# A fused decoder layer on one core: the second tile's softplus moved to the next batch's first quarter, and the prologue's rotation, loads and copies put in another order

## The chip, the cores and the metric

One core of a Trainium2 chip runs the whole program. The metric is the device time of one execution in microseconds (us); lower is better. The engines are TensorE (PE, its weight loads PEld), VectorE (DVE), ScalarE (ACT), GpSimd (POOL) and SyncE (SP, which only issues DMAs here). Each runs its own list of instructions in program order and waits on semaphores.

## What is computed

Four sequences of 512 tokens with 512 features go through three blocks, each followed by a sum with its input and a layer norm: linear attention in chunks of 128, a selective scan (state space model) that is driven by a context, and a mixture of 64 experts.

```python
x = _layernorm(x + _L0_attn_ref(x, Wq, Wk, Wv, Wo, rms_w))
x = _layernorm(x + _L0_xattn_ref(ctx_1024, x, ...))
x = _layernorm(x + _L0_ffn_ref(x, router_weight, gate_up_proj, down_proj))
...
# inside _L0_xattn_ref, u = silu(conv(in_proj(ctx)) + conv_b)
dt_low, Bm, Cm = jnp.split(x_proj_w @ u, [dt_rank, dt_rank + d_state], axis=1)
dt = jax.nn.softplus(dt_proj_w @ dt_low + dt_proj_b)
state = state * exp(dt * A) + (dt * u) * b      # for each of 512 steps, 512 channels, 16 states
y = sum_n(state * c) + D * u
```

## The kernel before

`mixers` does attention, scan and routing; `experts` runs behind it, from about 760 us on, and isn't touched.

The work of `mixers` is staged in batches b (4) and quarters c (4 in each batch, so t = 4b + c counts 16 quarters). A quarter does one tile of 128 channels of the scan, one chunk of attention, and pieces of other work that are placed between the scan's units by hand. The 512 channels of u are four tiles m = 0..3; quarter c scans tile c. A quarter has 8 units k, and unit n = 32b + 8c + k covers four states of 64 channels in two groups: POOL multiplies dt*u by B into `dbu` (`inputs`, L1122), ACT makes exp(dt*A) into `hst` (`decays`, L854), VectorE scans twice (L1312) and multiplies by C (L1318), TensorE sums the states into `y_ps` (`sum_states`, L426).

Units of half a tile share one spread: `copy_steps` (L399) waits for `dtu_ready`, then issues eight DMAs that copy dt and dt*u from `made` into one of two `rep` buffers, four for each of two groups of rows. `decays` and `inputs` of a spread's first unit wait until all of them have landed (`copied`). All copies are issued by SP, but for the second group of the very first spread, which ACT issues.

dt of a tile is a softplus, in steps that go from engine to engine: `project_dt` (TensorE, L455), `soften` (ACT, L874 and L876), `exponentials` (L883, L886), `rounded` (L896), `logs` (L892), `soft_parts` (two POOL instructions, L1128 and L1129), `excess` (ACT, L900), `soft_rest` (POOL, L1134), `steps` (ACT, L904, a ramp), `steps_of_u` (POOL, L1140, dt*u, which raises `dtu_ready`). For b >= 1 tiles 0 and 1 (EARLY) are made in the last quarter of the batch before, tiles 2 and 3 (LATE) in quarters 0 and 1 of their own. For batch 0 tile 0 is made in the prologue, its last steps on VectorE (`first_steps`, L1347 to L1359), and tile 1 in quarter 0.

TensorE's results other than `y_ps` go through three PSUM buffers used in turn (`to_fill`): the use number k waits until the use k - 3 has been emptied. The prologue is written out: four products of the context, the first tap, convolution and SiLU that give u, q0, the product of u (`project_u`), dt of tiles 0 and 1, k0, v0; POOL rotates q0 and k0 (`rotate`, L1195 to L1199), TensorE turns them (L476), ACT copies the result (`qT0`, `kT0`) and makes the first decays.

## Time and profile before

| | us |
|---|---|
| median of 3 runs | 1326.63 |
| lowest, highest | 1321.89, 1329.96 |
| the profiled execution, its own time | 1328.6 |
| its span, first to last instruction | 1326.8 |

| engine | busy us | share |
|---|---|---|
| PE | 1141.6 | 86% |
| DVE | 1112.4 | 84% |
| POOL | 969.8 | 73% |
| ACT | 848.2 | 64% |

The engines' shares are over the whole span; `experts` is 567 us of it. The mean granted clock of TensorE is 0.889 of 2.4 GHz. Starts of scans are the best clockwork of `mixers`: the first scan of a quarter is unit 8c + 0, and the first scans of the batches start at 46.23, 208.79, 383.08 and 564.85 us.

### The profile page before, as it was taken

Reading aid. Unit: us, or ns where it says so; the run is one execution under the profiler, and the core shown is the slowest. Engines: PE = TensorE matmul, PEld = TensorE weight load, DVE = VectorE, ACT = ScalarE, POOL = GpSimd, SP = SyncE. Lnnn points to the kernel's source line nnn. Section 1 sums busy time; section 2 is a strip of 40 time slices with the busy share of each in tenths; the row PEclk is TensorE's granted clock in tenths of the full one; section 3 lists DMA queues with packets and bytes.
Section 4 is the critical chain, followed back from the end, with each engine's and each line's share of the span. In section 5 each row is a group of like instructions: output and inputs, shape, how many; then the busy total and the mean of one; then the engine's idle time right before and its main releaser. Section 6 shows DMA issues by size and latency. Waiting matters only on the chain. (4 is left out here: it accounts for less than half of the span.)

```text
span 1326.8 us, 19363 instructions
## 1 busy us (share of the span) xinstructions
PE 1141.6 (86%) x6421; PEld 764.8 (58%) x6421; DVE 1112.4 (84%) x1564; ACT 848.2 (64%) x1522; POOL 969.8 (73%) x760
## 2 busy tenths in 40 slices
PE   8579998899978979887897749999999999999950
PEld 3334333444433533344443439999989999999940
DVE  3679998989978899788899658998988988988947
ACT  5564585745756446566345338888878888888833
POOL 0688678978999998999895224877767777777644
PEclk9689998898979879887987659999999999999985
DMA  8337326332253332243322337999999999999988
GB/s 303 77 80 240 73 60 158 111 79 54 54 139 80 112 84 49 65 112 111 72 53 96 100 103 215 315 304 308 299 297 305 307 291 305 301 302 311 288 137 333
DMA packets 95138, 235.03 MB, mean 177 GB/s; under 512 B 18608, under 2 KB 18864, under 8 KB 94400
## 3 DMA queue, kind: packets, MB, share of 16 engines
q1 hardware_dynamic: 64128, 161.92, 40.5%
q0 software_dynamic: 30720, 71.36, 22.6%
q8 instruction: 52, 0.85, 0.3%
q10 hardware_dynamic: 192, 0.52, 0.2%
q14 instruction: 46, 0.38, 0.1%
HBM read 147.33 MB, written 52.85 MB: 151 GB/s over the span
## 5 line engine op out<-in xcount | busy, mean ns | idle before, releaser
L1122 POOL TENSOR_TENSOR dbu<-rep,bc 128x1024 f32<-128x1024 f32 x128 | 303.0, 2370 | 62.2 <-PE y_ps L426 27.3
L1312 DVE TENSOR_TENSOR_SCAN hst<-hst,dbu 128x512 f32<-128x512 f32 x256 | 299.1, 1214 | 53.2 <-POOL dbu L1122 42.7
L1786 POOL DMA_INDIRECT sum_rows<-ye,tokens x128 | 204.5, 1598 | 101.0 <-ACT ye L1862 78.7
L1778 POOL DMA_INDIRECT xe<-x_rows,tokens x128 | 152.2, 1189 | 74.8 <-issue 37.8
L426 PE MATMUL y_ps<-dbu,cs 128*32 128x512 f32 x512 | 157.5, 699 | 55.6 <-DVE dbu L1318 43.6
L854 ACT ACTIVATE hst<-rep,small_sb 128x512 f32<-128x512 f32 x256 | 165.9, 685 | 54.5 <-DVE dbu L1318 43.0
L464 PE MATMUL ring<-first_raw,xT 128*128 128x512 f32 x384 | 177.7, 607 | 1.0 <-DVE x L1399 1.0
L1318 DVE TENSOR_TENSOR dbu<-hst,bc 128x1024 f32<-128x1024 f32 x128 | 156.7, 1224 | 4.4
L1828 PE MATMUL low<-xh,w1h 128*128 128x256 f32 x512 | 150.8, 295 | 0.0
L1828 PE MATMUL low<-xl,w1h 128*128 128x256 f32 x512 | 145.5, 284 | 0.0
L1828 PE MATMUL low<-xh,w1l 128*128 128x256 f32 x512 | 145.4, 284 | 0.0
L464 PEld LDWEIGHTS ring<-first_raw,xT 128*128 128x128 f32 x384 | 70.1, 192 | 97.1 <-issue 97.1
L1938 DVE TENSOR_TENSOR w1l<-first_raw,w1h 128x1024 fp32r<-128x1024 f32 (+1 forms) x128 | 117.0, 956 | 9.8 <-ACT w1h L1880 1.2
L1931 DVE TENSOR_TENSOR xl<-turn,xh 128x512 fp32r<-128x512 f32 x128 | 82.6, 686 | 32.8 <-ACT xh L1872 31.8
L1880 ACT ACTIVATE w1h<-first_raw 128x1024 fp32r<-128x1024 f32 (+1 forms) x128 | 101.0, 844 | 5.6 <-PEq L160 5.6
L1828 PEld LDWEIGHTS low<-xl,w1h 128*128 128x128 f32 x512 | 99.0, 193 | 0.0
L1828 PEld LDWEIGHTS low<-xh,w1l 128*128 128x128 f32 x512 | 98.8, 193 | 0.0
L1828 PEld LDWEIGHTS low<-xh,w1h 128*128 128x128 f32 x512 | 98.8, 193 | 0.1
L426 PEld LDWEIGHTS y_ps<-dbu,cs 128*32 128x32 f32 x512 | 20.2, 115 | 120.6 <-DVE dbu L1318 56.5
L485 PEld LDWEIGHTS ring<-qT,kT 32*128 32x128 f32 x512 | 47.7, 272 | 62.8 <-ACT qT L829 33.3
L1816 PE MATMUL turn<-cs,xe 128*128 128x128 f32 x512 | 68.8, 278 | 14.1 <-DMA xe<-x_rows,tokens 13.3
L1195 POOL TENSOR_TENSOR rot<-qk,cs 128x512 f32<-128x512 f32 x32 | 40.4, 1284 | 52.0 <-ACT qk L829 52.0
(208 smaller groups left out, 2726.6 us busy)
## 6 DMA issues: line engine op xcount, KB each, us to landing
first_raw<-in_gate_up SPq DMA_DIRECT2D x64, 768.0 KB, 9.8
rep<-made SPq DMA_DIRECT2D x252, 128.0 KB
second_raw<-in_down SPq DMA_DIRECT2D x64, 256.0 KB, 5.5
bc<-bc_rows SPq DMA_DIRECT2D x64, 128.0 KB, 3.1
second_raw<-in_down SPq DMA_DIRECT2D x64, 128.0 KB, 7.4
rows<-sum_rows SPq DMA_DIRECT2D x16, 512.0 KB, 9.6
sum_rows<-x2T SPq DMA_DIRECT2D x1, 4608.0 KB, 16.6
xT<-in_x_turned SPq DMA_DIRECT2D x16, 256.0 KB, 3.1
```

Source lines behind the costliest of these rows:

```text
L426: ins = pe.matmul(y_ps[rows, :], sel, dbu[:, n % WORK, g, :], start=(k == 0), stop=(k == QUADS - 1))
L464: ins = pe.matmul(ps[:, :], xT[:, t % 2, k, :], wqkv[:, "qkv".index(name), k, :], start=(k == 0), stop=(k == KD - 1))
L854: act.activation(hst[:, at % HBANKS, :], rep[:, i % 2, g, 0, :], ACT.Exp, scale=a_sc[:, 4 * m + 2 * half + g, k:k + 1]).then_inc(da_ready, 1)
L1122: pool.tensor_tensor(dbu[:, n % WORK, :, :], rep[:, i % 2, :, 1, :], bc[:, k, 0, :].unsqueeze(1).broadcast_to([P, 2, T]), ALU.mult).then_i ...
L1312: dve.tensor_tensor_scan(h, h, dbu[:, n % WORK, i, :], 0.0, ALU.mult, ALU.add).then_inc(scanned, 1)
L1318: dve.tensor_tensor(dbu[:, n % WORK, :, :], hst[:, first:first + 2, :], bc[:, k, 1, :].unsqueeze(1).broadcast_to([P, 2, T]), ALU.mult).the ...
L1778: pool.indirect_dma_start(xe[:, e % RAW, j, :], None, x2_dram, bass.IndirectOffsetOnAxis(ap=tokens[:, e, j:j + 1], axis=0))\
L1786: pool.indirect_dma_start(sum_dram[e % SUMS], bass.IndirectOffsetOnAxis(ap=tokens[:, e, j:j + 1], axis=0), ye[:, e % YE, j, :], None, comp ...
L1828: ins = pe.matmul(dst, w[:, s, k, at:at + P], x[:, s, k, :], start=(k == 0 and n == 0), stop=(k == KD - 1 and n == 2))
L1880: act.activation(w1h[:, e % 2, :, cols], w1[:, e % RAW, :, cols], ACT.Copy).then_inc(w1h_ready, 1)
L1931: dve.tensor_tensor(xl[:, e % 2, :, cols], turn_ps[j][:, :].rearrange("p (k t) -> p k t", k=KD), xh[:, e % 2, :, cols].bitcast(F32), ALU.s ...
L1938: dve.tensor_tensor(w1l[:, e % 2, :, cols], w1[:, e % RAW, :, cols], w1h[:, e % 2, :, cols].bitcast(F32), ALU.subtract).then_inc(w1l_ready, 1)
```

## The change

- TensorE's prologue makes q0 behind the product of u and dt of tiles 0 and 1, and ACT copies q0 out behind the first softplus.
- POOL waits for the first `dtu_ready` before it rotates q0 and k0.
- SP waits for two taps (`tapped`) before it issues the second turned tile of x, the first two tiles of x and wo.
- SP issues all eight copies of the first spread; ACT issues none.
- For b >= 1, five POOL instructions and two of ACT for tile 1 go elsewhere. `soft_parts` goes from POOL's step k = 5 of the batch before's last quarter to k = 0 of quarter 0, `soft_rest` from k = 7 to k = 4 of quarter 0, `steps_of_u` from k = 0 to k = 5 of quarter 0, and ACT's `excess` and `steps` into quarter 0 as well. That is the order that batch 0 already has, but for `soft_parts` at k = 0 instead of 2.

```diff
@@ -399,18 +399,6 @@
-        def copy_steps(eng, b, m, half, groups):
...
-            for g in groups:
...
@@ -602,9 +590,9 @@
             for m in range(MI):
                 project_context(0, m)
-            project(0, "q")
             project_u(0)
             project_dt(0, EARLY)
+            project(0, "q")
             project(0, "k")
             project(0, "v")
@@ -733,6 +721,17 @@
+            def copy_steps(b, m, half):
+                i = spread_of(b, m, half)
+                sp.wait_ge(dtu_ready, softened(b, m))
+                wait(sp, da_ready, 2 * QUADS * (i - 1))
+                wait(sp, dbu_ready, QUADS * (i - 1))
+                for g in range(2):
+                    rows = slice((2 * half + g) * QP, (2 * half + g + 1) * QP)
+                    for s in range(4):
+                        sp.dma_start(rep[s * QP:(s + 1) * QP, i % 2, g, :, :], made[rows, PLACES[m], :, :])\
+                            .then_inc(copied[i % 2], 16)
@@ -767,6 +766,7 @@
             sp.dma_start(dmask[:, :, :], dmask_in).then_inc(mask_loaded, 16)
+            sp.wait_ge(tapped, 2)
             load_turned(1)
             load_x(0)
             load_x(1)
@@ -774,7 +774,7 @@
-            copy_steps(sp, 0, 0, 0, (0,))
+            copy_steps(0, 0, 0)
@@ -951,17 +951,16 @@
             gate_u(0)
-            take("q0", flat(qk[:, 0:HEADS, :]))
             take("xdbl0", xdbl[:, :])
             soften(0, (0,))
             act.wait_ge(set_up, 1)
             exponentials(0, (0,))
             rounded(0, 0)
             logs(0, (0,))
+            take("q0", flat(qk[:, 0:HEADS, :]))
             take("k0", flat(qk[:, HEADS:, :]))
             soften(0, (1,))
             take("v0", v[:, :])
-            copy_steps(act, 0, 0, 0, (1,))
             take("qT0", flat(qT[:, :, :]))
@@ -1022,7 +1021,8 @@
                     if t == 0:
                         weigh_rows()
-                        excess(0, 1)
+                    if c == 0:
+                        excess(b, 1)
@@ -1057,9 +1057,8 @@
                         take(f"k{t + 1}", flat(qk[:, HEADS:, :]))
-                    if t == 0:
-                        steps(0, 1)
                     if c == 0:
+                        steps(b, 1)
                         exponentials(b, LATE)
@@ -1069,7 +1068,6 @@
                     if soft:
                         steps(b + 1, 0)
-                        excess(b + 1, 1)
@@ -1088,8 +1086,6 @@
-                    if soft:
-                        steps(b + 1, 1)
@@ -1229,6 +1225,7 @@
             pool.wait_ge(set_up, 1)
+            pool.wait_ge(dtu_ready, 1)
             rotate(0)
             inputs(0)
@@ -1244,14 +1241,12 @@
-                        if k == 0 and c == 0 and b:
+                        if k == (0 if b else 2) and c == 0:
+                            soft_parts(b, 1)
+                        if k == 4 and c == 0:
+                            soft_rest(b, 1)
+                        if k == 5 and c == 0:
                             steps_of_u(b, 1)
-                        if k == 2 and t == 0:
-                            soft_parts(0, 1)
-                        if k == 4 and t == 0:
-                            soft_rest(0, 1)
-                        if k == 5 and t == 0:
-                            steps_of_u(0, 1)
@@ -1272,9 +1267,6 @@
                         if k == 5 and c == NT - 1 and not last:
                             soft_rest(b + 1, 0)
-                            soft_parts(b + 1, 1)
-                        if k == 7 and c == NT - 1 and not last:
-                            soft_rest(b + 1, 1)
```

TensorE, start of the program, before: q0 is row 2 (first_raw holds the weights of q, k and v), the product of u row 3, dt of two tiles row 4.

```order
1 L435 MATMUL ring<-ctxT,second_raw 128x512 x8
2 L464 MATMUL ring<-first_raw,xT 128x512 x4
3 L445 MATMUL ring<-u_sb,small_sb 48x512 x4
4 L455 MATMUL ring<-xdbl,dt_wT 128x512 x2
5 L464 MATMUL ring<-first_raw,xT 128x512 x8
```

Now:

```order
1 L423 MATMUL ring<-ctxT,second_raw 128x512 x8
2 L433 MATMUL ring<-u_sb,small_sb 48x512 x4
3 L443 MATMUL ring<-xdbl,dt_wT 128x512 x2
4 L452 MATMUL ring<-first_raw,xT 128x512 x12
```

q0 has moved behind rows 3 and 4 and stands with k0 and v0.

POOL, around the first dbu of batch 1 (row 87 before), before. `made<-made,acc` and `ctxT<-made,ctxT` are `soft_parts`, `made<-made,ctxT` is `soft_rest`, `made<-made,u_sb` is `steps_of_u`:

```order
77 L1134 TENSOR_TENSOR made<-made,ctxT 128x512
78 L1128 TENSOR_TENSOR made<-made,acc 128x512
79 L1129 TENSOR_TENSOR ctxT<-made,ctxT 128x512
80 L1150 TENSOR_SCALAR rms<-ssq 128x1
81 L1152 TENSOR_TENSOR rms<-rms,half_sb 128x1
82 L1140 TENSOR_TENSOR made<-made,u_sb 128x512
83 L1122 TENSOR_TENSOR dbu<-rep,bc 128x1024
84 L1195 TENSOR_TENSOR rot<-qk,cs 128x512 x2
85 L1198 TENSOR_TENSOR qk<-rot 128x32x8
86 L1199 TENSOR_TENSOR qk<-rot 128x32x8
87 L1122 TENSOR_TENSOR dbu<-rep,bc 128x1024
88 L1134 TENSOR_TENSOR made<-made,ctxT 128x512
```

Now, from the same `soft_rest` of tile 0:

```order
77 L1130 TENSOR_TENSOR made<-made,ctxT 128x512
78 L1146 TENSOR_SCALAR rms<-ssq 128x1
79 L1148 TENSOR_TENSOR rms<-rms,half_sb 128x1
80 L1136 TENSOR_TENSOR made<-made,u_sb 128x512
81 L1118 TENSOR_TENSOR dbu<-rep,bc 128x1024
82 L1191 TENSOR_TENSOR rot<-qk,cs 128x512 x2
83 L1194 TENSOR_TENSOR qk<-rot 128x32x8
84 L1195 TENSOR_TENSOR qk<-rot 128x32x8
85 L1118 TENSOR_TENSOR dbu<-rep,bc 128x1024 x2
```

Rows 78, 79 (`soft_parts` of tile 1) and 88 (`soft_rest`) are gone from here; `steps_of_u` of tile 0 and the rotation stand closer.

POOL, first quarter of batch 1, before: `steps_of_u` of tile 1 is row 94, the rotation of the next chunk rows 100 to 102.

```order
93 L1209 TENSOR_TENSOR kdec<-qk,cs 128x512
94 L1140 TENSOR_TENSOR made<-made,u_sb 128x512
95 L1122 TENSOR_TENSOR dbu<-rep,bc 128x1024 x2
96 L1145 TENSOR_TENSOR y<-y,x 128x512 x2
97 L1122 TENSOR_TENSOR dbu<-rep,bc 128x1024 x3
98 L1150 TENSOR_SCALAR rms<-ssq 128x1
99 L1152 TENSOR_TENSOR rms<-rms,half_sb 128x1
100 L1195 TENSOR_TENSOR rot<-qk,cs 128x512 x2
101 L1198 TENSOR_TENSOR qk<-rot 128x32x8
```

Now:

```order
89 L1205 TENSOR_TENSOR kdec<-qk,cs 128x512
90 L1124 TENSOR_TENSOR made<-made,acc 128x512
91 L1125 TENSOR_TENSOR ctxT<-made,ctxT 128x512
92 L1118 TENSOR_TENSOR dbu<-rep,bc 128x1024 x2
93 L1141 TENSOR_TENSOR y<-y,x 128x512 x2
94 L1118 TENSOR_TENSOR dbu<-rep,bc 128x1024 x2
95 L1130 TENSOR_TENSOR made<-made,ctxT 128x512
96 L1118 TENSOR_TENSOR dbu<-rep,bc 128x1024
97 L1136 TENSOR_TENSOR made<-made,u_sb 128x512
98 L1146 TENSOR_SCALAR rms<-ssq 128x1
99 L1148 TENSOR_TENSOR rms<-rms,half_sb 128x1
100 L1191 TENSOR_TENSOR rot<-qk,cs 128x512 x2
```

`soft_parts` stands where `steps_of_u` was; `soft_rest` and `steps_of_u` of tile 1 stand ahead of the root (`rms`) and the rotation.

## Rows read from the trace of the kernel before

**Rows 1.** The page, costliest groups (count, busy us, mean ns, idle us before, releaser)
```profile
L1122 POOL TENSOR_TENSOR dbu<-rep,bc 128x1024 f32<-128x1024 f32 x128 | 303.0, 2370 | 62.2 <-PE y_ps L426 27.3
L1312 DVE TENSOR_TENSOR_SCAN hst<-hst,dbu 128x512 f32<-128x512 f32 x256 | 299.1, 1214 | 53.2 <-POOL dbu L1122 42.7
```

**Rows 2.** Busy time by stretches (us, then PE, PEld, DVE, ACT, POOL with counts, PEclk, DMA)
```profile
330.94:380.69 49.75, 44.28 (x190) 18.27 (x189) 42.27 (x43) 31.98 (x51) 46.17 (x37) 0.96 0.30 69
380.69:412.19 31.50, 27.62 (x144) 13.70 (x142) 26.44 (x28) 18.41 (x30) 29.25 (x22) 0.79 0.54 129
...
204.90:237.31 32.41, 26.84 (x148) 13.92 (x146) 27.95 (x30) 18.45 (x30) 24.69 (x20) 0.84 0.56 134
```

**Rows 3.** The same view, of stretches in the prologue and first quarter
```profile
11.60:25.00 13.40, 12.72 (x30) 4.52 (x28) 8.13 (x16) 7.47 (x11) 0.00 (x0) 1.00 0.86 346
25.20:28.50 3.30, 3.30 (x5) 1.42 (x5) 0.57 (x1) 3.24 (x5) 0.00 (x0) 0.50 0.61 177
...
38.90:59.20 20.30, 10.61 (x64) 6.46 (x68) 12.87 (x14) 12.62 (x17) 14.83 (x8) 0.50 0.40 91
```

**Rows 4.** Timeline of TensorE, prologue (start us, us, engine, line, tiles, idle before)
```profile
15.55 3.67 PE L464 MATMUL ring<-first_raw,xT 128*128 128x512 f32 x8
19.15 3.63 PE L445 MATMUL ring<-u_sb,small_sb 128*48 128x512 f32 x8
23.46 2.14 PE L455 MATMUL ring<-xdbl,dt_wT 16*128 16x512 f32 x4 [0.68 <-ACT xdbl L829]
```

**Rows 5.** Timeline of ACT and its DMA queue, prologue
```profile
17.73 1.95 ACT L869 ACTIVATE u_sb<-acc,small_sb 128x512 f32<-128x512 f32 x3
19.89 0.72 ACT L869 ACTIVATE u_sb<-acc,small_sb 128x512 f32<-128x512 f32 x1 [0.21 <-DVE acc L1335]
...
24.62 0.69 ACT L874 ACTIVATE acc<-ring,small_sb 128x512 f32<-128x512 f32 x1 [1.21 <-PE ring L455]
...
36.36 3.88 ACTq L411 DMA_DIRECT2D rep<-made  x4
```

**Rows 6.** Timeline of VectorE, end of the first softplus and first scan
```profile
31.38 0.69 DVE L1350 TENSOR_TENSOR ctxT<-made,ctxT 128x512 f32<-128x512 f32 x1 [2.76 <-ACT ctxT L892]
32.18 1.63 DVE L1353 SCALAR_TENSOR_TENSOR made<-ctxT,made 128x512 f32<-128x512 f32 x1
33.84 1.36 DVE L1356 TENSOR_SCALAR made<-made 128x512 f32<-128x512 f32 x1
35.24 1.09 DVE L1359 TENSOR_TENSOR made<-made,u_sb 128x512 f32<-128x512 f32 x1
46.23 2.35 DVE L1312 TENSOR_TENSOR_SCAN hst<-hst,dbu 128x512 f32<-128x512 f32 x2 [9.90 <-POOL dbu L1122]
```

**Rows 7.** Timeline of POOL, first rotation and first dbu
```profile
32.00 2.92 POOL L1195 TENSOR_TENSOR rot<-qk,cs 128x512 f32<-128x512 f32 x2 [31.57 <-ACT qk L829]
...
43.85 4.64 POOL L1122 TENSOR_TENSOR dbu<-rep,bc 128x1024 f32<-128x1024 f32 x2 [6.95 <-DMA rep<-made]
```

**Rows 8.** Timeline of POOL, end of batch 1 and first quarter of batch 2
```profile
370.26 1.26 POOL L1129 TENSOR_TENSOR ctxT<-made,ctxT 128x512 f32<-128x512 f32 x1
...
372.43 1.26 POOL L1140 TENSOR_TENSOR made<-made,u_sb 128x512 f32<-128x512 f32 x1
...
380.69 2.35 POOL L1122 TENSOR_TENSOR dbu<-rep,bc 128x1024 f32<-128x1024 f32 x1 [0.81 <-DMA rep<-made]
...
412.19 2.51 POOL L1195 TENSOR_TENSOR rot<-qk,cs 128x512 f32<-128x512 f32 x2 [0.81 <-ACT qk L829]
...
422.23 2.35 POOL L1122 TENSOR_TENSOR dbu<-rep,bc 128x1024 f32<-128x1024 f32 x1
```

**Rows 9.** Timeline of ACT, copy of k in the first quarter of batch 2
```profile
411.46 0.60 ACT L829 ACTIVATE qk<-ring 128x512 f32<-128x512 f32 x1 [4.12 <-PE ring L464]
```

**Rows 10.** Timeline of VectorE, first and ninth scan of batch 2
```profile
383.08 2.35 DVE L1312 TENSOR_TENSOR_SCAN hst<-hst,dbu 128x512 f32<-128x512 f32 x2 [3.45 <-POOL dbu L1122]
...
424.61 2.35 DVE L1312 TENSOR_TENSOR_SCAN hst<-hst,dbu 128x512 f32<-128x512 f32 x2
```

14 lines of the change are left out of this document (3 added, 11 removed).

## The prediction

> **What bounds the kernel now.** I read the page first, then TensorE's clock by stretches, then the timelines of the prologue and of one passage from a batch to the next. The scan runs over 128 units. In each, GpSimd makes one product dbu (2370 ns) and VectorE runs two scans and one multiplication [rows 1]. VectorE is busy 84% of the span, and the page's biggest single wait inside the scan is of a scan for POOL's dbu: the two engines take turns in being late. The table by stretches says where [rows 2]. Around the passage from one batch to the next (330.94 to 380.69, 380.69 to 412.19) POOL is busy 46.2 of 49.8 us and 29.3 of 31.5 us, and most of the rest is issuing of scatters. Only in the first passage (204.90 to 237.31, where no scatter is issued yet) has it slack: 24.7 of 32.4 us. So two questions decide: how early the first scan starts, since nothing overlaps the chain before it, and whether POOL gets less to do where it is the bound. The expert stage from 760 us on is not touched.
>
> **Prologue, the chain before.** The four tiles of u are ready one after the other, the first at 17.73 + 0.65 = 18.4, the last at 19.89 + 0.72 = 20.6 [rows 5]. TensorE works on q0 from 15.55 to 19.2, on the product of u from 19.15 to 22.8, and on the first dt product from 23.46 [rows 4]. The softplus starts on ACT at 24.62 [rows 5]; VectorE's last instructions of it begin at 31.38, 32.18, 33.84 and 35.24 and end at 36.33 [rows 6]. Copies of dt and dt*u then land; POOL's first dbu starts at 43.85 [rows 7], 7.5 us later, and the first scan at 46.23 [rows 6].
>
> **Part 1, q0 behind the products of u and dt.** The product of u (8 passes) no longer waits for q0. It cannot end before the last u: 20.6 plus two passes at 3.63/8 = 0.45 each and the tail of a pass, about 21.9 instead of 22.8, a gain of 0.9. But TensorE now idles from 15.7 to 18.4. What the rows show of its clock: it was granted in full from 11.6 to 25.0, then half (1.2 GHz) from 25.2 to 28.5, after short idle time and products that use 16 rows, and half again from 38.9 to 59.2, after an idle stretch [rows 3]. I expect a fall here too, for one stretch as long as the row from 25.2 (3.3 us), in which about four passes cost twice 0.43: +1.7. Net +0.8. Bounds: -0.9 without a fall, +3.4 when all eight passes and both of the first dt product run at half (8 x 0.86 from 18.4 gives 25.3, +2.5, and 2 x 0.43 more).
>
> **Part 2, the rotation waits.** POOL rotates q0 and k0 from 32.00 on (2.92 for its first two instructions, some 2 more for the last two), beside VectorE's last three instructions, which take 1.63, 1.36 and 1.09 us; the same size of tile takes 0.69 at 31.38, before POOL started [rows 6, 7]. After the change POOL waits until dt*u is done, so these three should take 3 x 0.69 = 2.07 instead of 4.08: -2.0 (between 0, if POOL isn't the reason, and -2.3). The Trainium skill (SBUF — State Buffer, Who interferes with whom) says that a VectorE instruction with both inputs in SBUF and a GpSimd instruction that reads SBUF exclude one another; these rows fit it. What is behind the new wait on POOL: the rotation (about 5 us), then the first dbu. The rotation ends near 40, the copies land near 42, so it is covered. But TensorE's turning of q and k and ACT's copies of them stand behind it, and ACT's first decays behind those. q, k and v now follow dt one after the other (3.7 each), and v also waits until ACT has emptied the second dt tile, behind its copy of k0. I get ACT's decays near 44.4, against a dbu ready at 44.5. This cover is 0.1 to 0.3 us thin; if it is gone, the slow-clock case below shows the price.
>
> **Part 3, one copy queue.** Before, four of the eight copies of the first spread were issued by ACT in 3.88 us [rows 5], and SP's copies of the next spread ran beside them: 7.5 us from dt*u to the first dbu. Where SP alone issues all eight, the first dbu follows 380.69 - 373.69 = 7.0 us behind dt*u [rows 8]: -0.5, and ACT is free. The Trainium skill (DMA: Bandwidth & Descriptors, Issuing engines are not separate DMA queues) says that more issuing engines save the time of issuing and nothing else. By that alone one queue would lose 3.88 / 2 = 1.9 us here, and the sum below would be 2.4 us later; the row of a passage decides against it, since there a single queue is no slower.
>
> **Part 4, loads later.** x tiles, the second turned tile and wo are issued after the second tap instead of at once. Nobody needs them before the first quarter's middle; the transfers ahead of them keep the engines busy till then. Nothing either way.
>
> Sum of the prologue: +0.8 - 2.0 - 0.5 = -1.7. First scan at 44.5 instead of 46.2; the first quarter has the same order as before, so this goes through to the end.
>
> **Part 5, the second tile's softplus in the next quarter, three times.** From POOL's last quarter of a batch go two instructions (the second of them at 370.26, 1.26 long, ending the pair's 2.5 us) ahead of the first tile's dt*u at 372.43 [rows 8]. dt*u then comes 2.5 us earlier, its copies too, and the next batch's first scan (383.08, which waited 3.45 us for POOL [rows 10]) with it: -2.5. But the same five instructions (5 x 1.27) now all stand in the next quarter, and POOL is full there. Followed through with durations from the rows: the first pair and the rest take the place of what left, so POOL is 2.5 early until the fifth step. There the remaining part (1.25) and dt*u of tile 1 (1.28) are new ahead of the rotation. dt*u waits for ACT's ramp (0.6), which stands behind ACT's copy of k. That copy was at 411.46 [rows 9] and is now at about 409.0; ramp until 410.1, dt*u until 411.4, the root (0.9) until 412.3. The rotation started at 412.19 before [rows 8]: no gain left. The dbu at 422.23 was needed at once (it ends at 424.58, the scan starts at 424.61 [rows 8, 10]), so the scans follow POOL again, at +0.1. In the first passage the slack of POOL doesn't help, since its rotation too waited for k (same steps, +0.1 to +0.2). Three times +0.1 gives +0.3; bounds from -7.5 (all three gains kept) to +8.
>
> **Sum.** -1.7 + 0.3 = -1.4: the profiled span 1326.8 becomes 1325.4, its run 1328.6 becomes 1327.2, and the median of the runs 1326.6 becomes 1325.2.
>
> **Rivals.**
> A. The gain at the passages stays. For it: POOL's wait of 0.8 us for k ahead of the rotation at 412.19 [rows 8, 9] could swallow part. Against: the ends computed above meet within 0.1 us. It gives 1326.6 - 1.7 - 7.5 = 1317.4.
> B. The clock stays at half through the products of u and the first dt. The Trainium skill (TensorE: Matmul & The Clock Gate, The HAM clock gate) has the slow level as the resting state that activity releases, which speaks for a fall in the new idle stretch. The first dt*u comes +3.4 - 2.0 late, and q, k, v run later still, so ACT's decays end last: k copied near 39.7, v 5 us later, turned q and k copied at 46.4, a table load and one decay 1.9: first scan at 48.4, +2.2. Total 1329.1.
> C. Slower: a passage gives nothing (copies, not POOL, end last there) while the quarter behind it pays 2.65 for the two instructions and the root ahead of the rotation, and 0.5 on ACT, whose ramp goes ahead of the exponentials that the sixth unit's decays wait for. It decides as soon as the first dbu of a batch is less than 0.1 us earlier. 3 x 3.15 = 9.4: 1326.6 - 1.7 + 9.4 = 1334.3. Against: copies start with dt*u, which moves by 2.5.
> D. The rotation isn't what makes VectorE's three instructions slow; they keep 4.08 us. Total 1327.2.
>
> **Chances.** Forecast 0.55, A 0.12, B 0.13, C 0.07, D 0.13. What a measurement can tell from no change is about 0.5%, 6.6 us: only A is beyond it on the fast side (0.12) and C on the slow side (0.07); 0.81 in between. The runs of before lie 8 us apart, so the forecast's own range is 1321 to 1329. From 1317 (A) to 1331 all but C and some scatter is held.
>
> **What the profile after would show.** First scan at 44 to 45 us. VectorE's three last instructions of the first softplus at 0.7 each. TensorE's products of u in part 0.85 apart. Each batch's first scan 2.5 us closer to the scans before it (the wait ahead of it stays near 3.4, since the scan before it moves as well), and the scan eight units later with none of this left. I am wrong if the scan at a batch's ninth unit is early too (A), if the first scan is beyond 46 (B, D), or if a batch's first scan doesn't move (C).

## The result and the profile after

The changed kernel takes 1339.9 us (median of 4 runs, 1337.5 to 1340.9) against 1326.5 for the kernel before (4 runs beside them): a ratio of 1.0081, 95% interval 1.0045 to 1.0117. It is 13 us slower, where I forecast 1.4 us faster and a range that ended at 1331. The profiled execution of the changed kernel is the fastest of its four and has a span of 1335.6 us (before 1326.8), so the traces below account for 8.8 of the 13 us. Medians here and below are over all executions of a kernel, while the ratios leave out those that took over 1.5% more than its fastest (three of 12 in e1 and in e13, two in e10, one in e8, and one in e14, which took 2727 us). All line numbers moved: the scan is L1304 now, POOL's dbu L1118, the rotation L1191.

The page's two largest groups of the scan, as [rows 1]: the work is the same, the idle time ahead of it 4.0 us (POOL's dbu) and 4.9 us (the scan) more.

```profile
L1118 POOL TENSOR_TENSOR dbu<-rep,bc 128x1024 f32<-128x1024 f32 x128 | 301.7, 2359 | 66.2 <-DVE hst L1304 26.5
L1304 DVE TENSOR_TENSOR_SCAN hst<-hst,dbu 128x512 f32<-128x512 f32 x256 | 299.2, 1214 | 58.1 <-POOL dbu L1118 46.4
```

The prologue did what it should. Timeline of VectorE after, as [rows 6]: the three last instructions of the first softplus take 0.69, 0.43 and 0.69 us, and the first scan starts at 44.18.

```profile
32.93 0.69 DVE L1345 SCALAR_TENSOR_TENSOR made<-ctxT,made 128x512 f32<-128x512 f32 x1
33.65 0.43 DVE L1348 TENSOR_SCALAR made<-made 128x512 f32<-128x512 f32 x1
34.12 0.69 DVE L1351 TENSOR_TENSOR made<-made,u_sb 128x512 f32<-128x512 f32 x1
44.18 2.35 DVE L1304 TENSOR_TENSOR_SCAN hst<-hst,dbu 128x512 f32<-128x512 f32 x2 [9.37 <-POOL dbu L1118]
```

**A ledger by quarters.** I read the start of the first scan of each quarter (8 units) from VectorE's timeline, and took each quarter's length, from its first scan to the next quarter's. "2.1" is the second quarter of batch 2: batches and quarters are counted from 0. "Last scan" is the last pair of scans. The table gives the length before and the difference of each kernel to it, in us. The column after is this section's subject; the others are experiments below.

| quarter | before | after | e1 start | e2 tile | e9 steps | e10 | e16 (=e10) | e11 |
|---|---|---|---|---|---|---|---|---|
| ahead of the first scan | 46.23 | -2.0 | -2.4 | -0.4 | 0.0 | -4.2 | -4.1 | -4.4 |
| 0.0 to 0.2 | 123.95 | -1.8 | -2.1 | -0.2 | 0.0 | -2.4 | -2.4 | -1.7 |
| 0.3 | 38.61 | -0.8 | -0.1 | -0.9 | -0.8 | +0.4 | -0.9 | +0.8 |
| 1.0 | 40.57 | +2.1 | +0.6 | +2.0 | +0.4 | +0.5 | -0.7 | -0.3 |
| 1.1 | 47.66 | +0.9 | 0.0 | +0.9 | 0.0 | 0.0 | 0.0 | 0.0 |
| 1.3 | 41.68 | -1.5 | 0.0 | -1.6 | -1.4 | -1.6 | -1.7 | +0.5 |
| 2.0 | 41.53 | +3.2 | 0.0 | +3.3 | +2.1 | +2.3 | +1.9 | -1.5 |
| 2.1 | 54.06 | +4.9 | 0.0 | +4.9 | 0.0 | -1.8 | +8.1 | -0.4 |
| 2.3 | 41.83 | -1.6 | -0.1 | -2.1 | -2.0 | -1.7 | -1.8 | +0.3 |
| 3.0 | 41.51 | +3.6 | 0.0 | +3.3 | +2.1 | +2.8 | +2.6 | -1.1 |
| 3.1 | 53.19 | +2.3 | -1.1 | 0.0 | +2.3 | -0.8 | +9.1 | +0.4 |
| 1.2, 2.2, 3.2, 3.3 | 166.04 | +0.5 | +3.1 | +0.2 | +0.4 | +0.8 | +0.8 | +0.8 |
| last scan to the end | 589.93 | -0.9 | +1.5 | -3.9 | +0.3 | +0.9 | +4.6 | -0.1 |

The changed kernel gets 3.9 us at its three passages (0.3, 1.3, 2.3) instead of 7.5, and pays 8.8 us in the first quarters and 8.1 us in the second quarters of batches 1 to 3. My sum had +7.8 in the first quarters, and nothing behind them.

Two cautions. The -1.8 us of 0.0 to 0.2 is not the change's: e4, e5 and e12, which have the prologue of before, show the same -1.7 there, and e2 and e9 do not (-0.2, 0.0). And three kernels were profiled twice (e1 and e13, e10 and e16, e11 and e18). From 1.1 to 1.3, in 2.0, in 2.3 and in 3.0 the two profiles of one kernel agree within 0.4 us; ahead of the first scan and in batch 0 they differ by up to 1.7 us, in 1.0 and behind 3.1 by up to 1.2, in 2.1 and 3.1 by up to 9.9, and behind the last scan by up to 3.7. So single numbers there have to be read with care.

**The passage** (timeline of POOL after, end of batch 1 and start of batch 2, as [rows 8]). The product dt*u starts at 368.57, directly behind the root, and ends at 369.83. That is 3.9 us earlier than before; 1.3 us of it were there at the start of this quarter already (the sum of the column after down to 1.2), and 2.5 us are the gain as forecast. But the first dbu starts 8.05 us behind dt*u's end, not 7.0, and the second one waits once more, for the B and C rows of k = 1, which stand behind the eight copies in SP's queue.

```profile
368.57 1.26 POOL L1136 TENSOR_TENSOR made<-made,u_sb 128x512 f32<-128x512 f32 x1
...
377.88 2.35 POOL L1118 TENSOR_TENSOR dbu<-rep,bc 128x1024 f32<-128x1024 f32 x1 [1.82 <-DMA rep<-made]
380.78 2.34 POOL L1118 TENSOR_TENSOR dbu<-rep,bc 128x1024 f32<-128x1024 f32 x1 [0.55 <-DMA bc<-bc_rows]
```

SP's queue, before and then after, shows where 1.1 us of it are: the eight copies are issued in 6.07 us instead of 4.96. The extra time is in one of the eight issues, the fifth, from 372.31 on: it took 1.71 us where the others take 0.6. POOL's rotation begins at 372.12. In the first passage, where no scatters are issued, no issue is that long.

```profile
373.71 4.96 SPq L411 DMA_DIRECT2D rep<-made  x8
```

```profile
369.85 6.07 SPq L732 DMA_DIRECT2D rep<-made  x8
```

**The first quarter** (POOL after, as the rotation at 412.19 in [rows 8]). The chain is the one I had followed: dt*u waits for ACT's ramp, then come root and rotation. Its durations are right: 3.4 us from the start of the key's copy to the rotation, forecast 3.3. Its place is not. The rotation is at 412.59 where I had put 412.3, but my 412.3 stood for Part 5 alone, and this trace is 1.3 us early from the quarters ahead; against that the rotation is 1.6 us later than forecast. The two numbers meet by luck. The key's copy (first row, ACT) waits for TensorE, and came 0.9 us earlier by this passage, not 2.5.

```profile
409.21 0.60 ACT L829 ACTIVATE qk<-ring 128x512 f32<-128x512 f32 x1 [4.11 <-PE ring L452]
```

```profile
410.41 1.28 POOL L1136 TENSOR_TENSOR made<-made,u_sb 128x512 f32<-128x512 f32 x1 [0.98 <-ACT made L904]
411.77 0.19 POOL L1146 TENSOR_SCALAR rms<-ssq 128x1 f32<-128x1 f32 x1
412.04 0.57 POOL L1148 TENSOR_TENSOR rms<-rms,half_sb 128x1 f32<-128x1 f32 x1
412.59 2.48 POOL L1191 TENSOR_TENSOR rot<-qk,cs 128x512 f32<-128x512 f32 x2
```

VectorE's last scans of that quarter then wait for POOL twice, and the ninth scan starts at 424.97 (before 424.61, [rows 10]; with the 1.3 us of the quarters ahead taken off, 1.7 us later).

```profile
420.23 2.35 DVE L1304 TENSOR_TENSOR_SCAN hst<-hst,dbu 128x512 f32<-128x512 f32 x2 [1.37 <-POOL dbu L1118]
...
424.97 2.35 DVE L1304 TENSOR_TENSOR_SCAN hst<-hst,dbu 128x512 f32<-128x512 f32 x2 [1.13 <-POOL dbu L1118]
```

**The second quarter of batch 2** loses most. Busy times by stretches, first the kernel before, then after (columns as in [rows 2]), each from the quarter's ninth scan: 0 to 20, 20 to 40 and 40 to 50 us. In the middle one TensorE is busy throughout in both, but its granted clock is 1.00 before and 0.84 after, and VectorE does 3.2 us less of its work. From 19.7 to 26.5 us into the quarter the clock is half after, and full before.

```profile
424.61:444.61 20.00, 14.05 (x86) 8.93 (x90) 15.14 (x16) 11.10 (x18) 19.10 (x19) 0.66 0.51 161
444.61:464.61 20.00, 19.92 (x113) 10.79 (x103) 16.95 (x29) 7.66 (x14) 17.93 (x15) 1.00 0.33 79
464.61:474.61 10.00, 6.98 (x25) 2.58 (x24) 9.79 (x18) 4.18 (x7) 9.13 (x7) 1.00 0.01 0
```

```profile
424.97:444.97 20.00, 13.54 (x79) 8.82 (x81) 15.14 (x16) 11.10 (x18) 19.10 (x19) 0.59 0.45 148
444.97:464.97 20.00, 19.92 (x109) 12.46 (x99) 13.79 (x30) 7.25 (x14) 14.81 (x12) 0.84 0.34 80
464.97:474.97 10.00, 10.00 (x32) 3.73 (x31) 9.79 (x19) 3.63 (x7) 9.22 (x9) 1.00 0.07 13
```

What this does to POOL: its rotation waits 3.53 us for ACT's copy of the key instead of 1.25, and starts 39.3 us into the quarter instead of 36.2 (before, then after). The scatters stand behind it, and the last one is issued 2.8 us later in the quarter.

```profile
460.78 2.66 POOL L1195 TENSOR_TENSOR rot<-qk,cs 128x512 f32<-128x512 f32 x2 [1.25 <-ACT qk L829]
```

```profile
464.29 2.48 POOL L1191 TENSOR_TENSOR rot<-qk,cs 128x512 f32<-128x512 f32 x2 [3.53 <-ACT qk L829]
```

The end of that quarter, VectorE after: an update of the slot numbers waits 5.27 us until the last scatter of the batch has landed. Before, that scatter landed just as VectorE came to it.

```profile
482.77 1.08 DVE L1458 TENSOR_SCALAR spill_f<-spill_f 128x32 f32<-128x32 f32 x1 [5.27 <-DMA slot_table<-tok_i,idx_s]
```

### The profile page after: what moved, and what is told of

Its sections match the earlier page's. It is cut to its first block and busy times, and to the rows that moved or that the text cites. A ratio compares the mean times of both kernels' runs of the same rounds, so it can differ in the third digit from the quotient of the medians.

```text
span 1335.6 us, 19363 instructions
## 1 busy us (share of the span) xinstructions
PE 1142.7 (86%) x6421; PEld 761.3 (57%) x6421; DVE 1110.5 (83%) x1564; ACT 847.8 (63%) x1522; POOL 966.5 (72%) x760
## 5 line engine op out<-in xcount | busy, mean ns | idle before, releaser
L1118 POOL TENSOR_TENSOR dbu<-rep,bc 128x1024 f32<-128x1024 f32 x128 | 301.7, 2359 | 66.2 <-DVE hst L1304 26.5
L1304 DVE TENSOR_TENSOR_SCAN hst<-hst,dbu 128x512 f32<-128x512 f32 x256 | 299.2, 1214 | 58.1 <-POOL dbu L1118 46.4
L414 PE MATMUL y_ps<-dbu,cs 128*32 128x512 f32 x512 | 160.3, 710 | 75.8 <-DVE dbu L1310 49.5
L1191 POOL TENSOR_TENSOR rot<-qk,cs 128x512 f32<-128x512 f32 x32 | 39.7, 1261 | 51.8 <-DVE made L1351 34.5
```

Of the source, the lines that this page charges most:

```text
L414: ins = pe.matmul(y_ps[rows, :], sel, dbu[:, n % WORK, g, :], start=(k == 0), stop=(k == QUADS - 1))
L1118: pool.tensor_tensor(dbu[:, n % WORK, :, :], rep[:, i % 2, :, 1, :], bc[:, k, 0, :].unsqueeze(1).broadcast_to([P, 2, T]), ALU.mult).then_i ...
L1304: dve.tensor_tensor_scan(h, h, dbu[:, n % WORK, i, :], 0.0, ALU.mult, ALU.add).then_inc(scanned, 1)
```

## Experiments

Theory 1: Part 5 costs the time, not the prologue. Within it, three causes were to be told apart: the order of the steps on the chain key copy, ramp, dt*u, rotation (theory O; its later form is theory C); POOL's sheer load in the first quarter (theory L); the scatters at the end of the second quarter (theory 1a). The rival to all of them: the shift of time by the prologue meets later waits in another way.

**e1_start and e2_tile: each half alone.** e1 undoes Part 5 in the changed kernel, e2 does it alone in the kernel before:

```diff
-                        if k == 0 and c == 0 and b:
-                            steps_of_u(b, 1)
-                        if k == 2 and t == 0:
-                            soft_parts(0, 1)
+                        if k == (0 if b else 2) and c == 0:
+                            soft_parts(b, 1)
...
```

> The kernel before with the changes of the prologue alone (Parts 1 to 4: products of u and dt ahead of the query's, the rotation behind the first dtu, one copy queue, later loads); the second tile's softplus stays in the last quarter of the batch before. Theory 1, the moved softplus is what costs the 13.4 us: this kernel is at or under the kernel before, 1322 to 1327 us (44.2 instead of 46.2 for the first scan, -2 us, if all of it reaches the end). Rival 2, the time shift of the prologue meets the waits of later quarters differently and that costs: 1335 to 1340 us. If half and half: 1331.

> The kernel before with Part 5 alone: for batches 1 to 3 the second tile's softplus in their first quarter, the prologue as before. Theory 1 (the move costs at each batch, and most in the second quarters of batches 2 and 3): 1336 to 1342 us, with the last scatter of the second quarter of batch 2 landing behind VectorE's use of it and a wait of some 5 us there. Rival 2 (the prologue's shift decides): 1325 to 1329 us. My own blind forecast of this part was +0.3 us.

e1: 1331.3 us, ratio 1.0012 (0.9988 to 1.0036). e2: 1335.4 us, ratio 1.0062 (1.0042 to 1.0083). Part 5 alone costs about 8 us, the prologue neither costs nor gains anything that these runs can tell, and the two ratios together make 1.0074, the changed kernel's within its interval. The ledger says the same quarter by quarter: quarters 1.0 to 2.1 of e2 and after agree within 0.2 us, and so does their loss of 4.9 us in 2.1, while e1 has 0.0 there. Theory 1 stands. How much of the 4.9 us in 2.1 belongs to Part 5 is less sure, as e4 and e15 will show.

**e3_send and e4_send_before: the wait for the last scatter.** On the kernels after and before:

```diff
-    return 2 if k >= UNIT - 2 else 1
+    return 0 if k == UNIT - 1 else 2 if k < 3 else 1
```

> The changed kernel with the 10 scatters of a batch's second quarter sent one unit earlier: two each in its first three units, one in the next four, none in its last (before: one in the first six, two in the last two). Theory 1a, the 5.27 us for which VectorE waits for the last scatter at 482.77 are lost time of their own: that wait goes, and the time falls by 3 to 5 us, to 1334 to 1337. Rival: GpSimd is late there in any case and the next wait takes its place (the first scan of the third quarter waits for GpSimd's product, or the earlier scatters delay GpSimd's rotation): within 1 us of the changed kernel, 1339 to 1341.

> The kernel before with the same earlier scatters. Theory 1a: its last scatter landed at 478.19, just as VectorE asked for it, so there is nothing to win, and the two more scatters ahead of the rotation cost GpSimd 1 us each at most: 1325 to 1329. If scatters as such slow what runs beside them, 1330 and more.

e3: 1337.5 us, ratio 1.0072 (1.0050 to 1.0094). The wait went; VectorE's timeline of e3 has the update at 479.86 without one, but two scans of the same quarter wait longer for POOL, behind the scatters sent earlier (1.62 and 4.54 us; in the kernel after 0.36 and 2.84):

```profile
438.49 2.35 DVE L1304 TENSOR_TENSOR_SCAN hst<-hst,dbu 128x512 f32<-128x512 f32 x2 [1.62 <-POOL dbu L1118]
447.97 2.35 DVE L1304 TENSOR_TENSOR_SCAN hst<-hst,dbu 128x512 f32<-128x512 f32 x2 [4.54 <-POOL dbu L1118]
...
479.86 0.18 DVE L1458 TENSOR_SCALAR spill_f<-spill_f 128x32 f32<-128x32 f32 x1
```

2.1 is 3.5 us shorter than after, and 3.1 is 7.0 us longer (there with TensorE's clock at half from 20 to 40 us into the quarter, of which more under e16). In the kernel before the same edit costs: 1333.0, ratio 1.0027 (1.0006 to 1.0047), where I had expected nothing. Its profile has 2.1 longer by 4.5 us and 3.1 by 3.7, of which the two moved scatters are 2.5 us each time (units 1 and 2), and in 2.1 TensorE's clock from 20 to 40 us into the quarter is 0.74. So 1a is right that the wait can go, but no gain in the whole shows (the intervals of e3 and of the kernel after overlap): a scatter moved ahead on POOL is paid where POOL is late. And e4 shows that a second quarter can lose over 4 us, partly by the clock, without Part 5.

**e5_turn_first: the rotation ahead of the subtraction and dt*u**, on e2 (batches 1 to 3):

```diff
-                        if k == 4 and c == 0:
+                        if k == 4 and t == 0:
                             soft_rest(b, 1)
-                        if k == 5 and c == 0:
+                        if k == 5 and t == 0:
                             steps_of_u(b, 1)
...
                             rotate(t + 1)
+                        if k == 5 and c == 0 and b:
+                            soft_rest(b, 1)
+                            steps_of_u(b, 1)
```

> The kernel with Part 5 alone, but in the first quarters of batches 1 to 3 GpSimd's rotation stands ahead of the second tile's last subtraction and its product with u, as it does in the kernel before. In the kernel with Part 5 alone the last two units of these quarters are 1.45 and 1.16 us longer than before (batches 2 and 3) and 0 and 1.14 (batch 1). Theory O, the order ahead of the rotation costs that (the step of my prediction that put 2.5 us there): these units are as long as before, within 0.3 us each. Theory L, GpSimd has work without a gap through the whole quarter, so that each microsecond moved into it comes out at its end whatever the order: both units together still 2.0 to 3.0 us longer.

It took 1351.3 us in a single run, 11.3 us of it in 2.1, with TensorE's clock at half from 20 to 40 us into that quarter. Neither theory had the rest: the last two units of the first quarters cost only +0.3 at most (as O), but the unit ahead of them 5.3 to 6.0 us. ACT's ramp (L904) waits for the subtraction (L1131), which now stands behind the rotation, which waits for ACT's copy of the key; and the decays of the next unit stand behind the ramp on ACT. Timeline of ACT in e5, batch 1:

```profile
234.15 0.60 ACT L829 ACTIVATE qk<-ring 128x512 f32<-128x512 f32 x1 [3.43 <-PE ring L464]
240.09 0.63 ACT L904 ACTIVATE made<-made 128x512 f32<-128x512 f32 x1 [5.35 <-POOL made L1131]
```

This pointed to the step in front. In e2 too the ramp (at 236.02 there) stands behind a copy that waits 3.43 us for TensorE, though its own input, the subtraction, ended at 227.93.

**e6_noscat_before and e7_noscat_tile: POOL's load.** The kernels before and e2 without their scatters (64 in the trace, about 1.0 us of POOL each; the expectation's 128 is a miscount).

> The kernel before without the 128 scatters of its slot table (and without the waits for them); its output is not the reference's. It is the base for the next kernel. Theory L: GpSimd gets 1.17 us per scatter, first quarters of batches 2 and 3 lose no more than 1 us, since VectorE is seldom behind GpSimd there; in all 1315 to 1327 us.

> Part 5 alone, without the scatters (output not the reference's). Theory L: without 7 us of scatters GpSimd has the room for the 3.8 us moved into the first quarter, so the last two units of the first quarters of batches 2 and 3 are within 0.5 us of the same kernel without Part 5 (with the scatters: +2.6), the second quarters are within 1 us (with them: +4.9 and 0), and the last scan starts 0 to 4 us later or up to 4 earlier instead of 9.6 later. Theory O (order or latency, not load): the first quarters are 2 us and more longer than without Part 5 here too, the last scan 6 us and more later.

1306.6 and 1314.2 us, a single run each, the first under what I had expected: Part 5 costs 7.5 us here too. The last scan starts 7.9 us later in e7 than in e6 (with scatters 9.6), but 1.8 us of that are in 0.0 to 0.2, where the two kernels are alike. The first quarters are +1.4, +1.7 and +0.8 us, the second ones +0.9 each. So the load of the scatters is not the only cause, and the 0.9 us of each second quarter come without it. It makes the loss larger: with scatters the first quarters of batches 2 and 3 lose 3.3 us, and 2.1 loses 4.9. The last units of all three first quarters now look alike (the eighth +1.1 us each), and like batch 1's in e2, which never had scatters there.

**e9_steps: the ramp ahead of the copies of query and key**, on e2. This is the edit that tells chain (C) from load (L):

```diff
                     take_squares(t)
+                    if c == 0 and b:
+                        steps(b, 1)
                     if soft or (back and c == 1):
                         take(f"q{t + 1}", flat(qk[:, 0:HEADS, :]))
...
-                    if c == 0:
+                    if t == 0:
                         steps(b, 1)
+                    if c == 0:
                         exponentials(b, LATE)
```

> Part 5 alone with one edit more: in batches 1 to 3 ScalarE's last step of the second tile (its Relu, for which GpSimd's product with u waits 3.32, 0.98 and 0.98 us in the first quarter) stands ahead of its copies of query and key instead of behind them. Theory C, the chain copy of the key, that step, product with u, root, rotation is what makes the end of the first quarter late, and through the rotation the second quarter of batches 1 and 2: last four units of batch 1's first quarter within 0.4 us of the kernel before (with Part 5 alone: +2.04), last two units of batches 2 and 3 within 0.8 us (+2.6), second quarters of batches 1 and 2 +0 to +0.3 and under +2 (+0.9, +4.9). Theory L (GpSimd is full, order is nothing): +1.5 to +2.6 stay in the first quarters.

First batch 1 of e2, where the chain is clearest. POOL waits 3.32 us for the ramp, and root and rotation follow:

```profile
236.72 1.28 POOL L1137 TENSOR_TENSOR made<-made,u_sb 128x512 f32<-128x512 f32 x1 [3.32 <-ACT made L904]
238.09 0.19 POOL L1147 TENSOR_SCALAR rms<-ssq 128x1 f32<-128x1 f32 x1
238.36 0.55 POOL L1149 TENSOR_TENSOR rms<-rms,half_sb 128x1 f32<-128x1 f32 x1
238.88 2.48 POOL L1192 TENSOR_TENSOR rot<-qk,cs 128x512 f32<-128x512 f32 x2
```

What POOL does behind the rotation is late with it. ACT (first row) waits 2.93 us for POOL's part of the fourth tile, with the copies of the turned query and key behind it, and VectorE (second row) waits 1.96 us for TensorE in the next quarter:

```profile
252.40 0.63 ACT L900 ACTIVATE ctxT<-ctxT 128x512 f32<-128x512 f32 x1 [2.93 <-POOL ctxT L1126]
```

```profile
256.19 1.29 DVE L1357 TENSOR_TENSOR pr<-ring,dmask 128x512 f32<-128x512 f32 x2 [1.96 <-PE ring L485]
```

In e9 the ramp runs at 232.65, the product with u no longer waits, the rotation waits for the key alone, and ACT's wait is back to 1.33. ACT (first two rows) and POOL of e9:

```profile
236.19 0.60 ACT L829 ACTIVATE qk<-ring 128x512 f32<-128x512 f32 x1 [2.91 <-PE ring L464]
...
250.47 0.63 ACT L900 ACTIVATE ctxT<-ctxT 128x512 f32<-128x512 f32 x1 [1.33 <-POOL ctxT L1129]
```

```profile
236.91 2.49 POOL L1195 TENSOR_TENSOR rot<-qk,cs 128x512 f32<-128x512 f32 x2 [0.72 <-ACT qk L829]
```

Batch 1: +0.4 and 0.0 instead of +2.0 and +0.9. Batches 2 and 3: the seventh unit +0.4 instead of +1.45, the second quarter of batch 2 0.0 instead of +4.9. Theory C holds for the first quarters and for batch 1's second. For 2.1 two profiles agree with it (e9 and e12, 0.0 each, clock 1.00), and e15 below does not, which has the mended ramp too and loses 11.7 us there: so that the 4.9 us come from the late rotation is likely, not shown. The eighth unit keeps its +1.17 (I had expected under 0.8 for the two), and this is the part of theory L: in e10, with one scatter less in that quarter, it is -0.06. 3.1 is +2.3 in e9, as in the kernel after: 2.9 us of it are one VectorE instruction that took 3.25 us beside a dbu of POOL (last section). The single run took 1331.9 us.

**e12_rows_first: the rows of k = 1 ahead of the copies**, on e9:

```diff
                             load_rows(b + 1, 0)
+                            load_rows(b + 1, 1)
                             copy_steps(sp, b + 1, 0, 0, (0, 1))
-                        if c == NT - 1 and k == 7 and not last:
-                            load_rows(b + 1, 1)
```

> The kernel of e9 with the rows of k = 1 of the next batch issued ahead of the eight copies instead of behind them. If the second scan of a batch waits for these rows alone: the second unit of the first quarters of batches 2 and 3 falls back to the kernel before (+0.74 and +1.24 with Part 5 alone, to 0), but the copies are issued 1.9 us later and the first scan with them: no gain in the sum, within 1 us of e9 at the last scan, or 3 us later. If the copies wait for nothing there, 2 us earlier.

1325.7 us, a single run. The second dbu follows the first without a wait now, and the first waits for its copies as long as in e9 (1.88 us): I expected four issues more ahead of the copies to delay them by 1.9 us, and they did not. Timeline of POOL in e12, then e9:

```profile
376.91 4.64 POOL L1121 TENSOR_TENSOR dbu<-rep,bc 128x1024 f32<-128x1024 f32 x2 [1.88 <-DMA rep<-made]
```

```profile
378.89 2.34 POOL L1122 TENSOR_TENSOR dbu<-rep,bc 128x1024 f32<-128x1024 f32 x1 [1.88 <-DMA rep<-made]
381.68 2.34 POOL L1122 TENSOR_TENSOR dbu<-rep,bc 128x1024 f32<-128x1024 f32 x1 [0.45 <-DMA bc<-bc_rows]
```

It is worth 0.5 us in each of the first quarters of batches 2 and 3.

**e8_mend and e10_two_mends: the mends in the changed kernel.** e8 has e9's step, the rows of k = 1 from ACT's queue, and other scatters; e10 the same with the rows in SP's queue:

```diff
-        return 2 if last else 1 if k < UNIT // 2 else 0
+        return 2 if last else 1 if k < UNIT // 2 or k == 6 else 0
     if c == 0:
-        return 1 if k < 6 else 0
-    return 2 if k >= UNIT - 2 else 1
+        return 1 if k < 5 else 0
+    return 0 if k == UNIT - 1 else 2 if k >= 4 else 1
```

> The changed kernel with three mends: ScalarE's last step of the second tile ahead of its copy of the query (GpSimd waited 0.98 us for it), the B and C rows of k = 1 loaded from ScalarE's queue at the passage instead of behind the eight copies in SP's (GpSimd waited 0.55 and 0.94 us), and of the scatters one moved from the first quarter into the gap behind the last quarter's rotation, and none in the last unit of the second quarter. Theory L: second unit of the first quarters 0.7 to 1.5 us shorter, its last two 1 to 2 us, and no wait of 5 us at the end of batch 2's second quarter: 1326 to 1332 us. Rival, the passage gives next to nothing and the loss comes back elsewhere: 1335 to 1340.

> The changed kernel with the step of e9 and the scatters of e8, and the rows of k = 1 in SP's queue again, since on ScalarE's queue they lost 2.35, 0.1 and 2.0 us in the second units of the first quarters. Theory C: the time is 3 to 5 us under e8's profiled course, the last scan starts at 727 to 731 us (kernel before: 736.86), and the median is 1318 to 1325. Rival, the ends of the scans do not carry to the end of the kernel, or the rows are late here as well: 1326 to 1332.

e8: 1329.2 (ratio 1.0021, 0.9986 to 1.0055). Another engine's queue was no help for the rows: ACT came to the four issues only behind its copy of v, which waited 5.70 us for TensorE; by then SP had issued the next rows and copies beside them, and POOL waited 3.52 us. (Not everywhere: 2.0 is 1.1 us shorter in e8 than in e10.) Timelines of ACT and POOL in e8, batch 1:

```profile
198.04 0.60 ACT L827 ACTIVATE v<-ring 128x512 f32<-128x512 f32 x1 [5.70 <-PE ring L452]
198.10 1.82 ACTq L1091 DMA_DIRECT2D bc<-bc_rows  x4
```

```profile
205.38 2.35 POOL L1126 TENSOR_TENSOR dbu<-rep,bc 128x1024 f32<-128x1024 f32 x1 [3.52 <-DMA bc<-bc_rows]
```

e10: its profiled run took 1323.7 us and its last scan started at 731.0, as expected, but its median is 1335.0 (1320.9 to 1344.1), ratio 1.0034 (1.0000 to 1.0069). The median misses the expectation (1318 to 1325). One profile could not explain that, hence e16.

**e16_two_mends_again: the kernel e10 once more.**

> The kernel e10 once more (its times ran from 1321 to 1344 at mean clocks of 0.900 down to 0.879). In a slow course the quarters that are longer are those in which TensorE's clock is lower than in e10's profile, and the time lost lies in one or two of the second quarters or behind the last scan, not in all of them by a little. In a fast course: 1321 to 1327 and nothing learned.

1344.4 us. The column in the ledger is the finding of this study that I had least expected: one program, two courses. All quarters agree with e10 within 1.3 us but 2.1 (+8.1 instead of -1.8) and 3.1 (+9.1 instead of -0.8); 3.7 us more lie behind the last scan. The stretches 20 to 40 us into 2.1, e10 first, then e16 (its first 20 us too):

```profile
439.54:459.54 20.00, 19.92 (x103) 10.61 (x94) 17.27 (x31) 8.55 (x16) 18.79 (x16) 1.00 0.32 79
```

```profile
416.84:436.84 20.00, 13.60 (x80) 8.66 (x80) 15.15 (x16) 11.10 (x18) 19.09 (x19) 0.64 0.49 158
436.84:456.84 20.00, 20.00 (x90) 13.25 (x83) 11.13 (x28) 5.25 (x10) 15.30 (x12) 0.50 0.32 79
```

TensorE is busy all of this stretch in both. In e10 it has the full clock (2.4 GHz), in e16 half (1.2 GHz), and VectorE does 11.1 us of work instead of 17.3. The first 20 us look alike: granted 0.66 and 0.64 in the mean, half from about 3 to 16 us. Then both go to full; in e10 it stays there, in e16 it falls again at 19.4 and is half until 39.9 us into the quarter. What I can show is this: in the second quarters of batches 2 and 3 the other engines wait for this stretch of TensorE, and in 2.1 the quarter's length follows its clock. It was 1.00 in before, e1 and e9 (54.0 us), 0.84 in after and e2 (58.9), 0.50 in e16 (62.1) and e15 (65.8). In 3.1 half the clock came with 5.7 us (e13, e15) to 9.3 us (e3) more, while 0.84 cost nothing that shows (53.2 us in before and e2, 54.3 at 1.00 in e12). Why a course takes the one or the other level is open.

**e11_gap and e18_gap_again: the first two steps in the gap of the passage.** On e10, soft_parts goes behind the last quarter's rotation:

```diff
-                        if k == (0 if b else 2) and c == 0:
+                        if k == 2 and t == 0:
                             soft_parts(b, 1)
...
                             rotate(t + 1)
+                        if k == 6 and c == NT - 1 and not last:
+                            soft_parts(b + 1, 1)
```

> The kernel of e10 with the first two GpSimd steps of the second tile (2.5 us) behind the rotation of the last quarter, where GpSimd waits 1.6 us for the copies anyway, instead of in the first quarter. Theory L: first scans of batches 0.5 to 1.2 us later, first quarters of batches 2 and 3 up to 2.5 us shorter: 1316 to 1324. Theory C, GpSimd's load in the first quarter costs little once the chain is mended: 1 to 3 us more than e10.

> The kernel e11 once more. If its gain is its own: ratio 0.993 to 0.998 again and a median under 1326. If it was luck with TensorE's clock in the second quarters: 0.999 to 1.004, with single runs over 1335.

e11: 1322.8 us (12 runs, 1319.8 to 1325.7), ratio 0.9957 (0.9937 to 0.9976). e18: 1322.6 (12 runs, 1319.5 to 1327.0), ratio 0.9960 (0.9942 to 0.9977). This kernel beats both, and none of its 24 runs is over 1327.0. Timeline of POOL in e11: the two steps and a scatter fill what was a wait for the copies.

```profile
371.11 0.72 POOL L1198 TENSOR_TENSOR qk<-rot 128x256 f32<-128x256 f32 x1
371.79 1.26 POOL L1127 TENSOR_TENSOR made<-made,acc 128x512 f32<-128x512 f32 x1
373.01 1.26 POOL L1128 TENSOR_TENSOR ctxT<-made,ctxT 128x512 f32<-128x512 f32 x1
374.45 1.06 POOL L1227 DMA_INDIRECT slot_table<-tok_i,idx_s  x1 [0.17 <-issue]
375.54 4.65 POOL L1121 TENSOR_TENSOR dbu<-rep,bc 128x1024 f32<-128x1024 f32 x2
```

The passages now give nothing (+0.8, +0.5, +0.3 against before), the first quarters gain 0.3, 1.5 and 1.1 us, and the chain ahead of the first scan 4.4 us.

**e15_gap_old_sends, e14_gap_old_start, e17_gap_rows_first: parts of e11 taken back or added.**

> The kernel e11 with the scatters spread as in the kernels before and after. If e11's gain comes from the mended move alone: 1321 to 1325. If from the scatters: the last unit of batch 2's second quarter is 3 to 6 us longer again and the first quarters' last units 1.2 us: 1327 to 1333.

> The kernel e11 without the prologue's changes (order of the query's products, the wait ahead of GpSimd's first rotation, one copy queue, later loads). If the prologue is worth 2 us: 1324 to 1326, first scan at 45.8 to 46.3. If it is worth nothing or costs: 1320 to 1323.

> The kernel e11 with the rows of k = 1 of the next batch issued ahead of the eight copies, as in e12, where it made the second unit of the first quarters of batches 2 and 3 0.5 us shorter. In e11 these units wait for nothing any more (-0.6 and 0.0 against the kernel before), so it adds nothing: within 1.5 us of e18. If the rows still come last: 1 us faster.

e15: 1333.7 us (1.0020, 0.9994 to 1.0045). With the scatters spread as before, e11's gain is gone, and e10 (the new scatters and the mended ramp, without the gap) does not have it either: neither edit is enough by itself. e15's profile has half the clock in 2.1 (+11.7 us) and in 3.1 (+5.7); I cannot tell how much of its distance to e11 is the scatters themselves and how much the clock. e14: 1327.0 (0.9951, 0.9914 to 0.9987), an interval that covers that of e11: no worth of the prologue shows. e17: 1323.0 (0.9967, 0.9950 to 0.9983), as expected no different from e18.

**e13_start_again: the prologue alone, a second time.**

> The prologue's changes alone, as e1, a second time. If they are worth the 1.7 us of my forecast: ratio to the kernel before 0.996 to 1.001 with e1's. If they bring TensorE's clock to fall more often in later quarters: 1.001 to 1.005 again, with runs from 1320 to 1344, and a profile in which a quarter is longer at a clock under 0.89.

1329.2 us (1321.6 to 1343.5), ratio 0.9973 (0.9939 to 1.0006). With e1's 1.0012 it straddles 1. The forecast of -1.7 us (0.9987) lies in this interval and just outside e1's; no effect at all lies in both. In its profile the first scan is 1.6 us early, and 3.1 is 5.7 us longer, with half the clock in the stretch named above. This is the size of luck that such a gain has to be seen against.

## Why the prediction was wrong, step by step

- **Parts 2 to 4** held: VectorE's three instructions took 1.81 us (I said 2.07) instead of 4.08, the first dbu came 7.0 us behind dt*u, and no wait for the later loads shows in the first 100 us. Rival D fell.
- **Part 1** held in size and as a mechanism: the product of u took 5.06 us with the clock falling for part of it (granted 0.59 from 18.50 to 22.00), and the first scan was at 44.18 for 44.5. In e11 the clock did not fall (1.00 over the same stretch, the product in 3.60 us), and its product also started 1.0 us earlier (17.48 instead of 18.47): the first scan was 4.4 us early instead of 2.0. With that start taken off, the product ended 0.7 us earlier than before, near my bound without a fall (-0.9); the upper bound (+3.4) never came. "This goes through to the end" isn't shown: in e1's profile the last scan is 2.0 us early, in e13's, the same kernel, 3.4 us late.
- **Part 5, the gain at the passage**: the term "-2.5" was -0.8, -1.5 and -1.6. dt*u did come as early as said. I took the 7.0 us from dt*u to dbu as fixed; it was 8.05 in batch 2, since the copies were issued 1.1 us more slowly, and the next unit waited 0.5 to 0.9 us for the rows of k = 1, which I had not followed though they stand in the same queue. For the first passage I have no test; that POOL had slack in that quarter (no scatters there), so that little was to be had, is an argument, and the profiles of one kernel differ there by 1.2 us.
- **Part 5, the first quarter**: the durations of "ramp until 410.1, dt*u until 411.4, the root until 412.3" were right, and so the loss of 2.6 us in the last two units of batches 2 and 3. What was wrong is where the chain begins: "that copy ... is now at about 409.0" takes the key's copy as 2.5 us early, and it was 0.9 us early. The net "+0.1" at the ninth scan was +1.3, +1.7 and +1.9: the passage gave 0.8 to 1.6 us, and the quarter took 2.1 to 3.6.
- **Part 5, the second quarter: the step that failed most.** I stopped at the ninth scan, and the three second quarters lost 8.1 us, more than the 3.6 us by which the three terms "-2.5" were too large. What I had moved stood ahead of the rotation, and behind the rotation stand dbu, the parts of the third and fourth tiles, ACT's turned query and key, and TensorE's products. That cost 0.9 us in batch 1 (e2, gone in e9). In batch 2 it was 4.9 us (e2, not there in e9): 0.9 of them come without scatters too (e7), the rest with TensorE's clock and the last scatter, and whether the late rotation brings the lower clock about is open. The 2.3 us of batch 3 are another thing: e2 has 0.0 there, and one VectorE instruction of 3.25 us (last section) explains them. My sum had no term for it, and the bounds -7.5 to +8 of Part 5 came from other ends: I gave +8, which leads to 1332.9 with the prologue's -1.7, and then let the range stop at 1331.
- **Rival C** gave 1334.3, the nearest of the cases to the measured 1339.9, and had 0.07. Its mechanism was half there: the quarter did pay 2.1 to 3.6 us (C: 3.15), but the passage gave half of what I had forecast, not nothing, and what came from behind the ninth scan C did not have. That its 9.4 us are near the 8 us of e2 is therefore in part luck. The chance was small because the sum closed to 0.1 us, and a sum of some ten steps, each good to some tenths, can't close like that three times over.

## What to carry to other kernels

A step that is moved drags its inputs along: on an in-order engine it must not stand behind a copy that waits for another engine when its own input has been there for long. One moved line on ACT (e9) took back 0.9 to 1.7 us in each of four quarters, and in its profile the 4.9 us of a fifth. Look for the moved work's place where its engine already waits for something else (e11, where the scatters had to be spread anew as well), and follow the chain at least one stage beyond the point where the first gain is used up. Before a gain of 2 us is believed, ask how far apart one program's own runs are: here 23 us (e10), and the two quarters that differ in the clock level make 20 us between its two profiles.
